# Moving the second layernorm's column sums into the loop over heads of a gated-scan block

## The reference, cut to what matters

```python
def block(x):                       # x: [8, 2048, 1024]
    # part 1: layernorm, rmsnorm, gated linear scan over the tokens
    h = rmsnorm(layernorm(x))
    q, kv, a = split(h @ w_qkva.T, 3)        # 3 x 1024 features
    a = sigmoid(a)
    y[t] = a[t] * y[t-1] + kv[t]             # scan along the tokens
    x = x + q * y
    # part 2: layernorm, soft mixture of 8 small experts
    h = layernorm(x)                         # mean and variance over features
    gate = softmax(h @ Wg + bg)              # 8 gates
    e_k = relu(h @ W1[k] + b1[k])            # 128 features each
    return x + sum_k gate[k] * (e_k @ W2[k] + b2[k])
```

## Time and profile before

| | |
|---|---|
| median of 11 runs | 521.5 us |
| profiled execution, its own time | 518.92 us |
| its span on the slowest core (core 6) | 517.4 us |
| spans of the 8 cores | 503.8 to 517.4 us |
| TensorE matmul busy | 404.8 us (78%) |
| VectorE busy | 236.8 us (46%) |
| ScalarE busy | 114.0 us (22%) |
| GpSimd busy | 102.0 us (20%) |
| table loads on ScalarE | 17 (16 of line 211, one of line 299) |
| mean granted TensorE clock, core 6 | 0.889 of 2.4 GHz |

### The profile page before, as it was taken

The page is one execution under the profiler, slowest core; times in us unless marked ns, Lnnn a source line. Parts: engine busy times, 40 slices in busy tenths (PEclk is TensorE's granted clock), DMA queues, the critical chain, the costliest instruction groups (busy, mean ns, idle before and its releaser), DMA issues.

```text
span 517.4 us, 4729 instructions; the slowest of 8 cores (503.8 to 517.4 us)
## 1 busy us (share of the span) xinstructions
PE 404.8 (78%) x1510; PEld 149.4 (29%) x1540; DVE 236.8 (46%) x356; ACT 114.0 (22%) x179; POOL 102.0 (20%) x76
## 2 busy tenths in 40 slices
PE   1434499834789999759879999779899998887894
PEld 0101144301222444213322444223233442232231
DVE  0264433443567344327376344447365344682221
ACT  1220001450124112610213112610232106202200
POOL 6000012402800022207300013219000123140000
PEclk9955789986588999977998999979889999998887
DMA  7999995082000000550300000630400000004004
GB/s 118 222 172 153 163 169 83 1 203 41 0 0 2 0 1 1 135 110 1 153 11 1 1 0 1 191 54 1 162 0 2 0 1 1 1 0 162 2 0 162
DMA packets 18231, 32.06 MB, mean 62 GB/s; under 512 B 656, under 2 KB 4752, under 8 KB 18208
## 3 DMA queue, kind: packets, MB, share of 16 engines
q0 software_dynamic: 9584, 14.98, 18.6%
q1 hardware_dynamic: 8624, 16.79, 10.0%
HBM read 38.35 MB, written 8.39 MB: 90 GB/s over the span
## 4 chain that ended last, share of the span: by engine, by line
PE 60%; DMA 17%; DVE 12%; issue 4%; ACT 2%; another core or an unknown queue 2%; POOL 1%; DVEq 0%; ACTq 0%; POOLq 0%
PE ps_kv L415 11%; PE ps_a L434 10%; PE ps_q L483 10%; DMA xbf<-xT 9%; PE ps_kv L718 8%; DMA wq_bf<-wqT 8%; PE ps_a L823 6%; PE ps_kv L823 3%; PE ps_a L718 3%; DVE rows L235 3%; PE ps_q L288 2%; PE ps_a L627 1%; PE ps_rep L768 1%; DVE wq_bf L199 1%
## 5 line engine op out<-in xcount | busy, mean ns | idle before, releaser
L506 POOL TENSOR_TENSOR x_sb<-x_sb,y_sb 128x512 f32<-128x512 f32 x32 | 40.5, 1265 | 271.4 <-DVE y_sb L494 271.3
L415 PE MATMUL ps_kv<-hbf,wq_bf 128*128 128x512 bf16 x248 | 66.6, 393 | 16.4 <-DVE carry L461 7.5
L434 PE MATMUL ps_a<-hbf,wq_bf 128*128 128x512 bf16 x252 | 62.8, 392 | 5.7 <-DVE wq_bf L199 5.5
L457 DVE TENSOR_TENSOR_SCAN y_sb<-asig,carry,ps_kv 128x512 f32<-128x512 f32 x24 | 30.7, 1280 | 62.5 <-ACT asig L446 62.5
L483 PE MATMUL ps_q<-hbf,wq_bf 128*128 128x512 bf16 x252 | 58.8, 379 | 0.2
L446 ACT ACTIVATE asig<-ps_a 128x512 f32<-128x512 f32 x32 | 19.1, 597 | 157.8 <-PE ps_a L434 153.2
L718 PE MATMUL ps_kv<-hbf,w_bf 128*128 128x512 bf16 x186 | 48.8, 410 | 3.8 <-DVE x_sb L837 3.2
L288 PE MATMUL ps_q<-xbf,statc 128*1 128x512 bf16 x32 | 13.1, 576 | 36.8 <-DMA xbf<-xT 36.8
L415 PEld LDWEIGHTS ps_kv<-hbf,wq_bf 128*128 128x128 bf16 x256 | 25.3, 99 | 54.0 <-issue 28.6
L434 PEld LDWEIGHTS ps_a<-hbf,wq_bf 128*128 128x128 bf16 x256 | 25.4, 100 | 37.8 <-issue 9.9
L823 PE MATMUL ps_a<-h1g,w_bf 128*128 128x512 bf16 x126 | 33.5, 412 | 0.4 <-issue 0.3
(11 more groups left out here) (82 smaller groups left out, 395.2 us busy)
## 6 DMA issues: line engine op xcount, KB each, us to landing
x_sb<-xT SPq DMA_DIRECT2D x4, 2048.0 KB, 14.5
outT<-x_sb SPq DMA_DIRECT2D x4, 2048.0 KB, 6.5
wq_bf<-wqT POOLq DMA_DIRECT2D x3, 2048.0 KB, 40.7
xbf<-xT POOLq DMA_DIRECT2D x3, 1024.0 KB, 17.3
w_bf<-w1p POOLq DMA_DIRECT2D x1, 2048.0 KB, 65.0
w_bf<-w2p POOLq DMA_DIRECT2D x1, 2048.0 KB, 76.8
xbf<-xT POOLq DMA_DIRECT2D x2, 512.0 KB, 12.6
wg_bf<-wgp POOLq DMA_DIRECT2D x1, 256.0 KB, 76.4
```

Source lines behind the costliest of these rows:

```text
L415: ii = tensor.matmul(ps_kv[:, j % 2, :], wq_bf[:, k, (8 + j) * 128:(9 + j) * 128], hbf[:, k, :], start=(k == 0), stop=(k == KC - 1))
L434: ii = tensor.matmul(ps_a[:, j % 2, :], wq_bf[:, k, (16 + j) * 128:(17 + j) * 128], hbf[:, k, :], start=(k == 0), stop=(k == KC - 1))
L457: s_dve.inc(vector.tensor_tensor_scan(y_sb[:, j, :], asig[:, j % 2, :], ps_kv[:, j % 2, :], init, ALU.mult, ALU.add))
L506: ii = gpsimd.tensor_tensor(x2buf(c)[:, j, :], x_sb[:, j, :], y_sb[:, j, :], ALU.add)
```

## The change

The casts, sums and squares of `emitC` are cut into pieces of one block and emitted inside stage B. `emit_cs(c, k)` emits the cast of block k, its sum on TensorE, and its square on ScalarE; it stands right behind `emit_q(c, k)`. `emit_s2b(c, k)` emits the sum of the squares of block k; in the loop it stands one head later, and for the last three blocks after the loop. The cast goes to `tbf` and is squared in place, so `hbf` is left to q; the two sums accumulate in `ps_rep` and no longer in `ps_q`. `emitRows2` keeps the row work, reading `ps_rep`. The next chunk's first column sum waits for the product of head 6 of this chunk, where it waited for the copy of the first row.

```diff
@@ emitS1
-                    tensor.wait_ge(s_dve.h, ck[c - 1]["mm_s2b_rdm"])
+                    tensor.wait_ge(s_dve.h, ck[c - 1]["attn"][KC - 2])
@@ emitB, loop over j and after it
                 if j >= 2:
                     emit_q(c, j - 2)
+                    emit_cs(c, j - 2)
+                if j >= 3:
+                    emit_s2b(c, j - 3)
             emit_q(c, KC - 2)
+            emit_cs(c, KC - 2)
             emit_q(c, KC - 1)
+            emit_cs(c, KC - 1)
+            emit_s2b(c, KC - 3)
+            emit_s2b(c, KC - 2)
+            emit_s2b(c, KC - 1)
@@ emitC is taken out; in its place
+        def emit_cs(c, k):
+            def _cast(scalar, k=k):
+                scalar.wait_ge(s_gp.h, K["x2"][k])
+                ii = scalar.activation(tbf[:, k, :], x2buf(c)[:, k, :], AF.Copy)
+            def _s1(tensor, k=k):
+                tensor.wait_ge(s_act.h, K["cast"][k])
+                ii = tensor.matmul(ps_rep[0:1, 0, :], statc[:], tbf[:, k, :],
+                                   start=(k == 0), stop=(k == KC - 1))
+            def _sq(scalar, k=k):
+                scalar.wait_ge(s_mm.h, K["mm_s1bk"][k])
+                ii = scalar.activation(tbf[:, k, :], tbf[:, k, :], AF.Square)
+        def emit_s2b(c, k):
+            def _s2(tensor, k=k):
+                tensor.wait_ge(s_act.h, K["sq2"][k])
+                ii = tensor.matmul(ps_rep[0:1, 1, :], statc[:], tbf[:, k, :],
+                                   start=(k == 0), stop=(k == KC - 1))
+        def emitRows2(c):
+            emit_rows(K, "mm_s2b", eps_add=1e-5, key_m="mm_s1b", pq=ps_rep)
+            emit_preload(AF.Exp)
@@ run_schedule
-                emitC(c)
+                emitRows2(c)
```

More of the change, by code:

```diff
@@ L213, in emit_preload, with emit_rows @@
             on("scalar", _pl)
-        def emit_rows(K, key, eps_add, key_m=None):
+        def emit_rows(K, key, eps_add, key_m=None, pq=None):
+            if pq is None:
+                pq = ps_q
             def _rows(vector):
                 vector.wait_ge(s_mm.h, K[key_m or key])
-                s_dve.inc(vector.tensor_copy(row(R_M), ps_q[0:1, 0, :]))
+                s_dve.inc(vector.tensor_copy(row(R_M), pq[0:1, 0, :]))
                 rec(K, key + "_rdm", s_dve)
@@ L225, in _rows @@
                 s_dve.inc(vector.scalar_tensor_tensor(row(R_S2), row(R_T0), -1.0,
-                                                      ps_q[0:1, 1, :], ALU.mult,
+                                                      pq[0:1, 1, :], ALU.mult,
                                                       ALU.add))
@@ L510, in emit_q @@
                 rec_i(K["x2"], j, s_gp)
-        def emitC(c):
+        def emit_cs(c, k):
             K = ck[c]
[L514 to L536, removed]
-            on("tensor", _s1)
[L538 to L545, removed]
-            on("scalar", _sq)
[L548 to L552, removed]
@@ new lines, in emit_cs @@
+            if state["counting"] and k == 0:
+                init(K, "cast")
+                init(K, "mm_s1bk")
+                init(K, "sq2")
+            def _cast(scalar, k=k):
+                scalar.wait_ge(s_gp.h, K["x2"][k])
+                ii = scalar.activation(tbf[:, k, :], x2buf(c)[:, k, :], AF.Copy)
+                s_act.inc(ii)
+            on("scalar", _cast)
+            rec_i(K["cast"], k, s_act)
+            def _s1(tensor, k=k):
+                tensor.wait_ge(s_act.h, K["cast"][k])
+                ii = tensor.matmul(ps_rep[0:1, 0, :], statc[:], tbf[:, k, :],
+                                   start=(k == 0), stop=(k == KC - 1))
+                s_mm.inc(ii)
@@ new lines, in emit_cs @@
+            on("tensor", _s1)
+            rec_i(K["mm_s1bk"], k, s_mm)
+            if k == KC - 1:
+                rec(K, "mm_s1b", s_mm)
+            def _sq(scalar, k=k):
+                scalar.wait_ge(s_mm.h, K["mm_s1bk"][k])
+                ii = scalar.activation(tbf[:, k, :], tbf[:, k, :], AF.Square)
+                s_act.inc(ii)
+            on("scalar", _sq)
+            rec_i(K["sq2"], k, s_act)
+        def emit_s2b(c, k):
+            K = ck[c]
+            def _s2(tensor, k=k):
+                tensor.wait_ge(s_act.h, K["sq2"][k])
+                ii = tensor.matmul(ps_rep[0:1, 1, :], statc[:], tbf[:, k, :],
+                                   start=(k == 0), stop=(k == KC - 1))
@@ L553, in _s2 @@
                 s_mm.inc(ii)
             on("tensor", _s2)
-            rec(K, "mm_s2b", s_mm)
-            emit_rows(K, "mm_s2b", eps_add=1e-5, key_m="mm_s1b")
+            if k == KC - 1:
+                rec(K, "mm_s2b", s_mm)
+        def emitRows2(c):
+            K = ck[c]
+            emit_rows(K, "mm_s2b", eps_add=1e-5, key_m="mm_s1b", pq=ps_rep)
             emit_preload(AF.Exp)
```

## The result

The changed kernel takes 690.9 us, the median of ten runs, against 520.6 us before, the median of 32: a ratio of 1.327, with a 95% interval from 1.323 to 1.331. In some runs of each kernel one die runs at a lower clock and the time is longer; all ratios and times here are of the other runs.

A forecast was written before the change was run, and what follows sets the result against it. TensorE was taken to bound stage B, and the next x transfer the gap between chunks. 4 x 28.6 - 3.7 = +110.7, with the clock +142.7, on 518.9, plus 2.6 carried over: 664 us, range 628 to 696.

The forecast's parts named there:

- TensorE's queue is held by the waiting sum: Stage B, after each q group: TensorE stands 3.78 us for the cast of that head's block; 28.6 us per chunk together.
- The full-clock step of 9.40 us: Stage B, from one sigmoid's start to the next: 9.40 us instead of 5.18 with TensorE at full clock.
- a clock that holds: Stage B: TensorE's clock does not fall in the stalls, so the time is 632 us; chance 0.08.
- The clock at 1.0 us per stall: Stage B: TensorE's clock falls at each of 8 stalls in 4 chunks, 1.0 us each, 32 us.
- Rival 2: Stage B: every stall brings a full low-clock group, 54 us instead of 32, so 687 us; chance 0.16.
- Nothing gained behind B in chunks 0 to 2: Behind stage B: the next chunk's bf16 x transfer ends last, not the statistics, so moving them gains nothing.
- Chunk 3: 12.5 to 8.8 us: Last x2 to broadcast in chunk 3, with no transfer behind it: 12.48 us becomes 8.8, gain 3.7.
- ScalarE and tables at nothing: Stage B: cast and square add 1.2 us per step on ScalarE, covered by its idle time; no table loads added.
- rival 3: Stage B: Square needs its own table, so sigmoids reload, 26 us more, 690 us (717 by the skill's switch); chance 0.10.
- Rival 4: Stage B: TensorE goes past the waiting sums, so the kernel is not slower, 500 us; chance 0.04.

The follow-up runs named there:

- the kernel with the filler: The changed kernel with 15 additional matmuls in front of each waiting sum, so TensorE works through most of the stall: 635.1 us, ratio 1.220.

## Why the prediction was right, and where it was off

- *TensorE's queue is held by the waiting sum.* Right: 3.5 us each in the trace, 3.66 in the working (six of 3.78, two of 3.29); one head later, 153 of the 170 us are gone; 1.39 us more in the chain, 52 us more in the time.
- *The full-clock step of 9.40 us.* Right: 9.46 with the clock held. The working gave 632 us for a clock that holds, and 635.1 was measured.
- *The clock at 1.0 us per stall.* This term failed by size: 1.74 by the two times, 1.6 by stage B of the two traces, which is 20 to 24 of the 27 us that were missing. The steps, forecast at 9.4 to 11 us, were 10.8 to 12.5. The rows gave 1.2 to 1.7, and the working went below them, as it assumed that part of each low stretch falls into the stall. The trace shows the fall near the stall's end (one microsecond before the end the granted clock was still 1.00 in 25 of the 32 stalls), and the low stretch on kv and a. Rival 2, with the full price of the rows, gave 687 and was the better sum. The Trainium skill ("HAM oscillation", TensorE: Matmul & The Clock Gate) tells of a kernel in which each burst after a wait starts on the low clock. This trace agrees in 23 of the 32 stalls, with 0.50 in the first 0.2 us behind the stall; in the other nine the clock fell within the next microsecond.
- *Nothing gained behind B in chunks 0 to 2.* Right: three transfers in the chain, and 36 us less once they were moved.
- *Chunk 3: 12.5 to 8.8 us.* 9.2 measured.
- *ScalarE and tables at nothing.* Right: 17 loads as before, so Square runs between the Sigmoids without a load, which rules out rival 3, and the casts alone are at 0.999.
- *Rival 4* found nothing for it: TensorE stood idle through all 32 waits of 3.5 us.
- *The rest of the 27 us.* In the profiled traces 3.6 us lie behind stage B of chunk 2: the broadcast starts 20.1 us after the last x2, and before it was 16.5, with a transfer of 16.45 us instead of 13.97. Why that transfer was quicker in the trace of before is not shown. About 2 us are hand-overs: stage B grew by 116.6 us in the four chunks of the kernel with the filler, and by 4 x 28.6 = 114.4 in the working.

## What to carry to other kernels

Before a small operation is moved into a loop on an in-order engine, count the chain from that engine's last feeding instruction round to the operation: it has to be shorter than the work that stands between. Here a wait of 3.5 us with nothing between, 32 times, and the clock that fell with it cost 170 us; the groups of one more head between them took back nine tenths. What stands behind a loop is worth moving only if it ends last there: ask first what else the next stage waits for, since here one transfer issued earlier gave 26 us, and only then did the rest of the tail count.

## What the runs showed of the hardware that was not expected

- 480 more matmuls made the kernel 56 us faster, as they held TensorE at 2.4 GHz in the stalls.
- The granted clock stayed at 1.00 until 258 in a stall from 255.4 to 259.3 and was at 0.50 behind it until past 264, so most of the low stretch lay on the work.
- One pair of one-column sums between 128-column groups took 0.63 us of TensorE and not the 0.43 that its 1024 columns stream in.
